# Layer 1 of a two-layer gated transformer: the last two batches as one pair instead of two single units

## The chip, the cores and the metric

The kernel runs on one core of a Trainium2 chip (trn2). The metric is the device time of one execution in microseconds (us), lower is better. The core has five instruction streams that run side by side: PE (TensorE, matrix products and transposes), DVE (VectorE), ACT (ScalarE), POOL (GpSimd) and SP (SyncE, which issues most DMAs). Each runs its own instructions strictly in the order in which they are written, and waits on semaphores that the others raise.

## The reference

Eight batches of 128 rows by 256 columns run through two layers. Cut to what matters here:

```
x = x + tanh(g_xattn[0]) * long_conv_mixer(ctx, ctx, layernorm(x))        # layer 0
x = x + tanh(g_ffn[0])   * routed_ffn(layernorm(x))                       # layer 0: router, 8 groups, silu(g) * u
x = x + tanh(g_xattn[1]) * attention(layernorm(x), ctx, mask)             # layer 1, "cross"
x = x + tanh(g_ffn[1])   * (relu(layernorm(x) @ T(w_fc))**2 @ T(w_proj))  # layer 1, "mlp"; T() = ternarized weight
```

The attention is `softmax(x ctx^T / 16 + mask) ctx`, with one head; the MLP has 640 hidden units. All is float32.

## The kernel before, in words

All of x stays on chip in the tile x_res (128 partitions = rows, then batch, then 256 columns). The work is cut into steps, such as `("down", 7)` or `("turn_1", 3)`, and every engine walks one common list of steps, `SCHEDULE`, and does its own part of each step. So the list sets the order on all engines at once. `make_schedule` builds the list: it has chains of steps (one chain per routine), each step has a number in the table `TIMES`, and the steps are sorted by it. The numbers are only sort keys, not times.

The steps that matter here:

- `warm n` lets PE do n products that nobody reads. `conv`, `fold`, `gather`, `kv` are the mixer of layer 0; `prod` is what DVE writes in a conv, `fold` is POOL's sum of it. `consts` needs the small tables (gates, the router's inverse map, mu) that SP loads.
- `chunk b c` (c = 0 to 3) are the up and gate products of the routed FFN of batch b: 12 products from line 679 and 2 from line 682. `turn_a b c` transposes the result; ACT copies it as a rounded part to a_t and DVE the remainder (`residue`, line 926). `down b` is 33 products (line 535) over the eleven tiles of a_t; the tiles 8 to 10 come from `turn_a b 3`. DVE adds the result to x_res (line 1184). Routers (`turn_top`, `flat`, `soft`, `turn_soft`) run once for each two batches, `tern_sum` belongs to the ternarized weights.
- Layer 1 runs in units, by the list `UNITS`: three pairs of batches, then batch 6 alone and batch 7 alone. A unit is a chain of 13 steps: `stat cross` (DVE statistics, POOL's rstd at line 1258), `norm cross` (DVE, xn, line 988), `turn_0` (PE transposes, ACT copies qt), `scores` (PE line 708; DVE lines 1194 and 1198; ACT exp, line 884), `turn_p` (PE, then ACT pt), `read` (PE line 720, DVE line 1209 into x_res), `stat mlp`, `norm mlp`, `turn_1` (PE, ACT rounded part and DVE remainder of x1t), `hidden` 0, 1, 2 (PE line 734; ACT relu line 904 and square line 909; DVE hsq line 1225 and the remainder hid_t line 1227), `out` (PE line 748, DVE line 1233 into x_res, then the store by SP, line 523).
- Almost each of these steps waits for the one ahead of it in its unit. `stat cross` of a unit waits for the `down` of its last batch. `hidden 0` of a unit may not stand before the `out` of the unit before it, since both use hid_t. PSUM has eight banks, given out in turn by `plan_psum`; after `down 7` five of them serve all steps.

The width of a step grows with the unit: with one batch, `hidden` has 20 products with 128 moving columns; with two it has 20 products with 256 columns:

```
                    n = P * len(UNITS[u])
                    for i, j in enumerate(range(2 * jp, min(2 * jp + 2, JT))):
                        for kt in range(2):
                            for part in range(2):
                                last = pe.matmul(psum(step)[:, i * n:(i + 1) * n],
                                                 fc_t[:, kt, j * P:(j + 1) * P], x1t[:, part, kt, 0:n],
```

Of the kernel before, what the change touches and what calls it, by code (L numbers as in the profile page):

```python
# [46 lines left out]
DONE_TILES = [range(0, 2), range(2, 5), range(5, 8), range(8, 11)]  # L47
WORDS = {"gate": 0, "up": 1}
TERNARY = ["fc", "proj"]
UNITS = [range(0, 2), range(2, 4), range(4, 6), range(6, 7), range(7, 8)]  # L50


RING_LOADS = ["gate0", "gate1", "gate2", "up0", "up1", "up2", "down0", "down1"]
# [6 lines left out]

WARMS = [13, 1, 0]
TIMES = {
    "weights": [92, 133, 137, 157, 169, 185, 211, 279, 279, 279, 281, 281, 281, 292, 296, 309, 313, 313, 327, 338,
        342, 358, 358, 358, 380, 391, 409],
    "consts": [105],
# [9 lines left out]
    "mask": [656],  # L77
    "ternary": [724, 760, 764, 807, 813, 838, 851, 863, 863, 867, 880, 921, 921, 946],
    "chunks": [547, 575, 592, 628, 656, 667, 698, 716, 736, 760, 784, 804, 836, 856, 888, 918, 924, 956, 972, 988,
        1008, 1034, 1034, 1054, 1068, 1094, 1100, 1120, 1137, 1160, 1170, 1192],  # L80
    "turns": [590, 593, 644, 660, 694, 704, 720, 740, 768, 796, 820, 844, 878, 900, 911, 927, 938, 980, 1000, 1008,
        1026, 1042, 1062, 1070, 1085, 1102, 1124, 1146, 1164, 1180, 1196, 1206],
    "downs": [689, 740, 844, 932, 1009, 1076, 1148, 1220],
# [9 lines left out]
}  # L93


def make_schedule():
# [7 lines left out]
    def router(r):  # L104
        return one_by_one((kind, "moe", r) if kind in ("stat", "norm") else (kind, r) for kind in (
            "stat", "norm", "turn_x", "logits", "top", "turn_top", "flat", "soft", "turn_soft"))

    def layer1(u):
        return one_by_one([("stat", "cross", u), ("norm", "cross", u), ("turn_0", u), ("scores", u), ("turn_p", u),
                           ("read", u), ("stat", "mlp", u), ("norm", "mlp", u), ("turn_1", u), ("hidden", u, 0),  # L110
                           ("hidden", u, 1), ("hidden", u, 2), ("out", u)])
# [24 lines left out]
    chains.update((f"router{r}", router(r)) for r in range(RUNITS))  # L136
    chains.update((f"unit{u}", layer1(u)) for u in range(len(UNITS)))
    timed = []
    for name, pieces in chains.items():
        timed += [(t, len(timed) + k, piece) for k, (t, piece) in enumerate(zip(TIMES[name], pieces, strict=True))]  # L140
        assert TIMES[name] == sorted(TIMES[name])
    start = [("warm", WARMS[0]), ("stat", "mix", 0), ("turn_ctx", 0, 0), ("turn_ctx", 0, 1), ("norm", "mix", 0),
             ("kv", 0, 0), ("warm", WARMS[1]), ("turn_q", 0, 0), ("turn_q", 0, 1), ("kv", 0, 1), ("warm", WARMS[2])]
    return start + [step for _, _, piece in sorted(timed) for step in piece]


def check_order(schedule):
# [5 lines left out]
    for b in range(B):  # L153
        for c in range(NCH):
            assert at["chunk", b, c] < at["turn_a", b, c]
        assert at["turn_a", b, NCH - 1] < at["down", b]
    for u, bs in enumerate(UNITS):
        assert at["down", bs[-1]] < at["stat", "cross", u]
# [23 lines left out]
def plan_psum():  # L182
# [19 lines left out]
    for i, step in enumerate(SCHEDULE):  # L202
        kind = step[0]
        if kind == "read":
            reads[kind] = len(UNITS[step[1]])
        if kind == "conv":
# [32 lines left out]
def batches_of(which, k):  # L239

    if which == "mix":
        return range(k * Q, (k + 1) * Q)
    return range(k * RQ, (k + 1) * RQ) if which == "moe" else UNITS[k]

# [15 lines left out]
def build(nc, x, ctx_rows, mask, g_xattn, g_ffn, kernel_rev, skip, gate_w, mask_up_w, gate_p, up_p, down_p, inv_map,  # L260
# [156 lines left out]
    def wait_drained(eng, key, reads=None):  # L417

        bank, _, before, n = USES[key]
        eng.wait_ge(drained[bank], before + (n if reads is None else reads))  # L420
# [50 lines left out]
    with block:  # L471

        @block.sync
        def _(sp):
# [39 lines left out]
            for n in range(3, len(RING_LOADS)):  # L514
# [5 lines left out]
                         w_proj.rearrange("(r p) j -> p r j", p=P)).then_inc(tern_loaded[1], 16)  # L520
            for u, bs in enumerate(UNITS):
                wait_drained(sp, ("out", u))
                sp.dma_start(out[bs.start:bs.stop].rearrange("b p l -> p b l"),
                             x_res[:, bs.start:bs.stop, :]).then_inc(stored, 16)
            sp.wait_ge(stored, 16 * len(UNITS))

# [789 lines left out]
```

## Time and profile before

| | before |
|---|---|
| median of 3 timed runs | 274.08 us (272.95 to 274.17) |
| the profiled execution, by the same clock as the runs | 271.08 us |
| its span in the trace (first to last instruction or landing) | 269.4 us |
| PE busy | 238.3 us (88%) |
| DVE busy | 184.8 us (69%) |
| ACT busy | 111.4 us (41%) |
| POOL busy | 73.4 us (27%) |
| mean TensorE clock granted, as a share of 2.4 GHz | 0.959 |

The profile is of one execution. All times inside it are counted from the start of its span. A busy share is an average over stages: what counts for a change is which engine is waited for in the stage in which it lies.

### The profile page before, as it was taken

The numbers are of one execution on the slowest core, as the hardware profiler recorded it, in microseconds if no ns is written. First come the engines' busy times: TensorE is split into PE (matmuls) and PEld (weight loads), VectorE is DVE, ScalarE is ACT, GpSimd is POOL, SyncE is SP. The second block draws the span as 40 slices with busy tenths as digits, with TensorE's granted clock in tenths as the row PEclk, the third lists the DMA queues.
The fourth block names the chain that finished last, engine by engine and source line by source line (L and its number), as shares of the span: only waits on it lengthen the run. The fifth ranks groups of instructions, "written<-read, shape, count | busy, mean of one in ns | idle before, by whom it ended". The sixth has DMA issues, their size and how long they took to land.

```text
span 269.4 us, 4600 instructions
## 1 busy us (share of the span) xinstructions
PE 238.3 (88%) x1580; PEld 225.3 (84%) x1580; DVE 184.8 (69%) x515; ACT 111.4 (41%) x229; POOL 73.4 (27%) x92
## 2 busy tenths in 40 slices
PE   7496789978789999999798799999999999996883
PEld 7495679868579998999788799999899999985873
DVE  2359999798995889686786484662764756685442
ACT  0602326840103263654444945373521771363331
POOL 1667687049586201000443110100011001102100
PEclk9889999999999999999799999999999999999566
DMA  4698527000000041000000000000000000101000
GB/s 159 190 350 191 156 58 217 1 0 1 4 0 0 2 134 63 0 1 2 0 0 2 0 0 4 1 2 0 0 24 17 2 0 4 39 0 39 4 19 19
DMA packets 14038, 11.50 MB, mean 43 GB/s; under 512 B 2912, under 2 KB 13760, under 8 KB 14016
## 3 DMA queue, kind: packets, MB, share of 16 engines
q1 hardware_dynamic: 13920, 11.16, 13.7%
q8 instruction: 13, 0.21, 0.3%
q10 hardware_dynamic: 96, 0.05, 0.1%
q14 instruction: 9, 0.07, 0.1%
HBM read 10.14 MB, written 1.07 MB: 42 GB/s over the span
## 4 chain that ended last, share of the span: by engine, by line
issue 39%; PE 30%; DVE 16%; POOL 7%; ACT 5%; DMA 1%; ACTq 0%; DVEq 0%; POOLq 0%
PE bank L679 10%; PE bank L535 6%; PE bank L542 3%; POOL kv L1280 2%; DVE prod L1007 2%; PE bank L580 2%; POOL rstd L1258 2%; DVE w_split L926 2%; PE bank L748 2%; PE bank L734 2%; ACT ctx_ext L757 2%; PE bank L582 2%; PE bank L581 2%; PE bank L682 2%; DMA x_res<-in_x 1%
## 5 line engine op out<-in xcount | busy, mean ns | idle before, releaser
L679 PE MATMUL bank<-w_split,xt 128*128 128x352 f32 x384 | 70.9, 334 | 0.0
L679 PEld LDWEIGHTS bank<-w_split,xt 128*128 128x128 f32 x384 | 62.7, 192 | 0.1
L1254 POOL TENSOR_SCALAR ve<-mv 128x2 f32<-128x2 f32 (+2 forms) x16 | 3.6, 227 | 149.2 <-DVE mv L966 149.2
L1173 DVE SCALAR_TENSOR_TENSOR act<-silu,scal,bank 128x176 f32<-128x176 f32 x64 | 22.6, 394 | 22.9 <-ACT silu L871 20.7
L535 PE MATMUL bank<-d_split,a_t 128*128 128x256 f32 x264 | 34.2, 286 | 0.0
L535 PEld LDWEIGHTS bank<-d_split,a_t 128*128 128x128 f32 x264 | 32.3, 191 | 0.5 <-DVE a_t L926 0.4
L871 ACT ACTIVATE silu<-bank 128x352 f32<-128x352 f32 x32 | 14.8, 464 | 35.2 <-PE bank L682 35.0
L1280 POOL TENSOR_TENSOR kv<-ctx_ext 128x880 f32<-128x880 f32 x16 | 27.5, 1720 | 3.0 <-ACT ctx_ext L757 2.2
L1291 POOL TENSOR_TENSOR fold<-prod 128x256 f32<-128x256 f32 x32 | 23.3, 742 | 18.3 <-DVE prod L1010 16.4
L580 PE MATMUL bank<-kv,toe 128*128 128x208 f32 x64 | 18.5, 371 | 9.5 <-DVE prod L1010 3.7
L580 PEld LDWEIGHTS bank<-kv,toe 128*128 128x128 f32 x64 | 10.6, 197 | 12.7 <-issue 9.7
L757 ACT ACTIVATE a_t<-bank 128x384 fp32r<-128x384 f32 (+1 forms) x32 | 14.7, 460 | 12.2 <-PE bank L542 11.9
L1007 DVE TENSOR_TENSOR prod<-bank,q_ext 128x320 f32<-128x320 f32 x32 | 15.5, 483 | 6.1 <-PE bank L582 4.8
L926 DVE TENSOR_TENSOR a_t<-bank,a_t 128x384 fp32r<-128x384 f32 (+1 forms) x32 | 16.6, 519 | 4.2 <-ACT a_t L757 3.9
L871 ACT ACT_TABLE_LOAD x10 | 12.8, 1283 | 12.9 <-PE bank L682 12.8
L988 DVE TENSOR_SCALAR xn<-x_res,mv,rstd 128x256 f32<-128x256 f32 x32 | 12.6, 438 | 6.5 <-POOL rstd L1258 6.5
L581 PE MATMUL bank<-kv,toe 128*128 128x208 f32 x64 | 16.8, 344 | 0.0
L582 PE MATMUL bank<-kv,toe 128*128 128x208 f32 x64 | 16.8, 344 | 0.0
L734 PE MATMUL bank<-x1t,fc_t 128*128 128x256 f32 (+1 forms) x100 | 16.3, 321 | 0.0
L682 PE MATMUL bank<-m_stack,soft_t 128*128 128x352 f32 x64 | 15.8, 328 | 0.0
L734 PEld LDWEIGHTS bank<-x1t,fc_t 128*128 128x128 f32 x100 | 15.2, 228 | 0.5 <-issue 0.3
L757 ACT ACTIVATE w_split<-bank 128x512 fp32r<-128x512 f32 (+1 forms) x12 | 6.4, 568 | 22.0 <-PE bank L542 22.0
(136 smaller groups left out, 425.8 us busy)
## 6 DMA issues: line engine op xcount, KB each, us to landing
toe<-lag_rows SPq DMA_DIRECT2D x4, 512.0 KB, 5.9
ring<-in_down_p SPq DMA_DIRECT2D x2, 704.0 KB, 4.9
x_res<-in_x SPq DMA_DIRECT2D x2, 512.0 KB, 4.4
ctx<-in_ctx_rows SPq DMA_DIRECT2D x2, 512.0 KB, 5.0
ring<-in_gate_p SPq DMA_DIRECT2D x2, 512.0 KB, 8.7
ring<-in_up_p SPq DMA_DIRECT2D x2, 512.0 KB, 4.5
out_x<-x_res SPq DMA_DIRECT2D x3, 256.0 KB, 2.2
tern_w<-in_w_fc SPq DMA_DIRECT2D x1, 640.0 KB, 4.2
```

What stands on the lines that cost most here:

```text
L535: last = pe.matmul(dst, lhs(a), rhs(b), start=start and i == 0, stop=stop and i == 2)
L580: pe.matmul(y[:, 0], toe[:, h, P:2 * P], pairs(0), start=True, stop=True)
L581: pe.matmul(y[:, 1], toe[:, h, 0:P], pairs(0), start=True, stop=False)
L582: fill(pe.matmul(y[:, 1], toe[:, h, P:2 * P], pairs(1), start=False, stop=True), step)
L679: pe.matmul(psum((name, b, c))[:, 0:CW], lhs, w_split[:, w, kt, part, cols], start=i == 0, stop=False)
L734: last = pe.matmul(psum(step)[:, i * n:(i + 1) * n], fc_t[:, kt, j * P:(j + 1) * P], x1t[:, part, kt, 0:n], start=kt + part == 0, stop=kt ...
L757: return act_e.activation(dst, src, ACT.Copy)
L871: drain(act_e.activation(silu[:, n % 2, :], psum(("gate", b, c))[:, 0:CW], ACT.Silu), ("gate", b, c))
L926: drain(dve.tensor_tensor(dst, src, hi.bitcast(F32), ALU.subtract), key)
L1173: drain(dve.scalar_tensor_tensor(out=act[:, g * NI:(g + 1) * NI], in0=silu[:, n % 2, cols], scalar=scal[:, b, g:g + 1], in1=psum(("up", b, ...
L1280: pool.tensor_tensor(kv[:, n % 2], view(ctx_ext, base, [[EXT, 4 * Q], [0, TAPS], [1, SPAN]]), view(ctx_ext, base, [[EXT, 4 * Q], [1, TAPS] ...
L1291: pool.tensor_tensor(f, p4[:, :, 0:4, :], p4[:, :, 4:8, :], ALU.add).then_inc(folded, 1)
```

## The change

`UNITS` gets four pairs. The two chains of single units become one chain of double width, and the sort keys are new, in the tail and, a little, elsewhere.

```
-UNITS = [range(0, 2), range(2, 4), range(4, 6), range(6, 7), range(7, 8)]
+UNITS = [range(0, 2), range(2, 4), range(4, 6), range(6, 8)]
...
-WARMS = [13, 1, 0]
+WARMS = [13, 0, 3]
 TIMES = {
...
-    "gather0": [84, 86, 146, 194, 223, 223, 288, 333],
+    "gather0": [64, 66, 146, 194, 223, 223, 288, 333],
...
-    "unit3": [1183, 1212, 1226, 1233, 1252, 1252, 1256, 1263, 1277, 1288, 1288, 1295, 1302],
-    "unit4": [1220, 1230, 1256, 1260, 1278, 1281, 1281, 1287, 1295, 1304, 1332, 1353, 1385],
+    "unit3": [1220, 1230, 1256, 1260, 1278, 1281, 1281, 1287, 1295, 1304, 1332, 1353, 1385],
 }
```

Apart from the tail, about a dozen pairs of neighbouring steps change places in the common list (three `turn_w` steps and one `turn_ctx` ahead of a conv or kv, `gather 0 0` ahead of the fourth conv, `turn_att 1 0` ahead of `logits 1`, `tern_sum fc` ahead of `chunk 2 1`, `stat moe 3` ahead of `chunk 2 2`, `hidden 1 2` ahead of `chunk 7 0`). The one source line that goes shifts all line numbers of the kernel after by one: line 748 of before is line 747 of after.

**The tail on PE.** From `down 7` (the 33 products with d_split and a_t) to the end, first before, where act is the routed FFN's result, xn_73 the normed rows of layer 1, s_att the attention weights, and each row has its count of products:

```order
L542 MATMUL bank<-ident,act 128x128 x3
L734 MATMUL bank<-x1t,fc_t 128x256 x4
L535 MATMUL bank<-d_split,a_t 128x256 x33
L542 MATMUL bank<-ident,xn_73 128x128 x2
L708 MATMUL bank<-ctx_ext,qt 128x128 x2
L748 MATMUL bank<-proj_t,hid_t 128x256 x20
L542 MATMUL bank<-ident,s_att 128x128
...
L734 MATMUL bank<-x1t,fc_t 128x128 x20
L542 MATMUL bank<-ident,xn_73 128x128 x2
L748 MATMUL bank<-proj_t,hid_t 128x256 x10
L734 MATMUL bank<-x1t,fc_t 128x128 x20
L748 MATMUL bank<-proj_t,hid_t 128x256 x10
```

and after:

```order
L733 MATMUL bank<-x1t,fc_t 128x256 x20
L541 MATMUL bank<-ident,act 128x128 x3
L534 MATMUL bank<-d_split,a_t 128x256 x33
L747 MATMUL bank<-proj_t,hid_t 128x256 x20
L541 MATMUL bank<-ident,xn_73 128x128 x4
L707 MATMUL bank<-ctx_ext,qt 128x128 x4
L541 MATMUL bank<-ident,s_att 128x128 x2
L719 MATMUL bank<-ctx,pt 128x256 x2
L541 MATMUL bank<-ident,xn_73 128x128 x4
L733 MATMUL bank<-x1t,fc_t 128x256 x20
L747 MATMUL bank<-proj_t,hid_t 128x256 x20
```

The two chains that were interleaved are one; the `out` of unit 2 (the first 20 products with proj_t) moved ahead of `turn_0`, and the last third of unit 2's `hidden` moved ahead of the last `turn_a`. (In the trace a product of two plain float32 operands, as in `scores`, `read` and the warm steps, counts as two records.)

**The tail on DVE, ahead of `down 7`.** This is the end of unit 2's `hidden` and the last remainder of a_t, which `down 7` needs; before:

```order
L1225 TENSOR_TENSOR hsq<-relu 128x512
L1227 TENSOR_TENSOR hid_t<-hsq,hid_t 128x2x256
L926 TENSOR_TENSOR a_t<-bank,a_t 128x3x128
L1225 TENSOR_TENSOR hsq<-relu 128x256
L1227 TENSOR_TENSOR hid_t<-hsq,hid_t 128x256
L988 TENSOR_SCALAR xn_73<-x_res,mv,rstd 128x256
L1184 SCALAR_TENSOR_TENSOR x_res<-bank,tg,x_res 128x256
```

and after:

```order
L1224 TENSOR_TENSOR hsq<-relu 128x512
L1226 TENSOR_TENSOR hid_t<-hsq,hid_t 128x2x256
L1224 TENSOR_TENSOR hsq<-relu 128x256
L1226 TENSOR_TENSOR hid_t<-hsq,hid_t 128x256
L925 TENSOR_TENSOR a_t<-bank,a_t 128x3x128
L1183 SCALAR_TENSOR_TENSOR x_res<-bank,tg,x_res 128x256
```

The remainder of a_t moved behind the last two operations of `hidden`, and the norm of the single batch 6 is gone from here.

**The middle on DVE.** This is the router of batches 4 and 5 around `tern_sum fc` (lines 1067 to 1071) and `flat 2` (from line 1135), before:

```order
L1062 TENSOR_REDUCE tern<-tern_w 128x1
L1173 SCALAR_TENSOR_TENSOR act<-silu,scal,bank 128x176 x2
L1067 TENSOR_SCALAR tern<-bank 128x1
L1070 TENSOR_SCALAR tern<-tern 128x1
L1071 TENSOR_SCALAR tern<-tern 128x1
L1135 TENSOR_REDUCE scal<-bank 128x16
```

and after:

```order
L1061 TENSOR_REDUCE tern<-tern_w 128x1
L1066 TENSOR_SCALAR tern<-bank 128x1
L1069 TENSOR_SCALAR tern<-tern 128x1
L1070 TENSOR_SCALAR tern<-tern 128x1
L1172 SCALAR_TENSOR_TENSOR act<-silu,scal,bank 128x176 x2
L1134 TENSOR_REDUCE scal<-bank 128x16
```

The three small operations moved ahead of the product of silu and up.

## Rows read from the trace of the kernel before

**Rows 1.** Timeline (start us, us): last down and unit 3's, unit 4's end.
```profile
237.10 4.12 PE L535 MATMUL bank<-d_split,a_t 128*128 128x256 f32 x33
239.09 0.55 DVE L926 TENSOR_TENSOR a_t<-bank,a_t 128x384 fp32r<-128x384 f32 x1
240.01 0.43 DVE L1227 TENSOR_TENSOR hid_t<-hsq,hid_t 128x256 fp32r<-128x256 f32 x1
241.26 0.48 DVE L1184 SCALAR_TENSOR_TENSOR x_res<-bank,tg,x_res 128x256 f32<-128x256 f32 x1 [0.50 <-PE bank L535]
242.46 2.65 PE L748 MATMUL bank<-proj_t,hid_t 128*128 128x256 f32 x20
250.42 1.22 PE L720 MATMUL bank<-ctx,pt 128*128 128x256 f32 x2 [0.59 <-ACT pt L757]
251.08 4.72 PE L734 MATMUL bank<-x1t,fc_t 128*128 128x128 f32 x20
264.17 2.50 PE L748 MATMUL bank<-proj_t,hid_t 128*128 128x256 f32 x10 [1.80 <-DVE hid_t L1227]
266.71 0.48 DVE L1233 SCALAR_TENSOR_TENSOR x_res<-bank,out_scale,x_res 128x256 f32<-128x256 f32 x1 [2.60 <-PE bank L748]
```

**Rows 2.** Half-microsecond windows of PE: length, busy (count), clock, DMA share, GB/s.
```profile
250.00:250.50 0.50, 0.08 (x1) 0.92 0.00 0
260.50:261.00 0.50, 0.50 (x6) 0.84 0.00 0
```

**Rows 3.** Timeline: steps of an earlier pair, unit 2, up to its norm.
```profile
214.72 1.08 PE L708 MATMUL bank<-ctx_ext,qt 128*128 128x128 f32 x8
216.12 0.41 DVE L1194 SCALAR_TENSOR_TENSOR s_att<-bank,neg 128x256 f32<-128x256 f32 x1
217.72 0.19 ACT L884 ACTIVATION_READ_ACCUMULATOR s_att<-s_att,nmax 128x1 f32 x1
223.01 1.03 PE L720 MATMUL bank<-ctx,pt 128*128 128x256 f32 x4
224.15 0.88 DVE L1209 SCALAR_TENSOR_TENSOR x_res<-bank,rv,x_res 128x256 f32<-128x256 f32 x2 [0.18 <-PE bank L720]
225.06 0.75 DVE L960 BATCH_NORM_STATS2 stats<-x_res 128x6 f32<-128x256 f32 x2
226.49 0.71 POOL L1258 TENSOR_TENSOR rstd<-ve,mhalf 128x2 f32<-128x2 f32 x1
227.81 0.73 DVE L988 TENSOR_SCALAR xn<-x_res,mv,rstd 128x256 f32<-128x256 f32 x2
```

**Rows 4.** Timeline: the same pair from turn_1 to the end of hidden.
```profile
231.30 0.60 PE L542 MATMUL bank<-ident,xn 128*128 128x128 f32 x4
234.31 2.15 PE L734 MATMUL bank<-x1t,fc_t 128*128 128x256 f32 x16
235.60 0.60 ACT L904 ACTIVATE relu<-bank 128x512 f32<-128x512 f32 x1 [0.46 <-PE bank L734]
236.30 0.69 DVE L1225 TENSOR_TENSOR hsq<-relu 128x512 f32<-128x512 f32 x1 [0.41 <-ACT relu L904]
```

**Rows 5.** DMA issues: tensor, queue, count, KB each, median us to landing.
```profile
out_x<-x_res SPq DMA_DIRECT2D x2, 256.0 KB, 2.2
out_x<-x_res SPq DMA_DIRECT2D x2, 128.0 KB, 1.7
```

**Rows 6.** Timeline: the router of batches 4 and 5.
```profile
125.00 0.71 DVE L1173 SCALAR_TENSOR_TENSOR act<-silu,scal,bank 128x176 f32<-128x176 f32 x2 [1.10 <-ACT silu L871]
126.17 0.29 DVE L1135 TENSOR_REDUCE scal<-bank 128x16 f32<-128x128 f32 x1
129.75 0.66 PE L542 MATMUL bank<-ident,soft_parts 128*128 128x128 f32 x4 [1.91 <-DVE soft_parts L1159]
130.50 3.48 PE L679 MATMUL bank<-w_split,xt 128*128 128x352 f32 x12
```

**Rows 7.** Timeline: the start, at the step consts.
```profile
22.58 0.20 ACT L767 ACTIVATE tg<-gates 128x4 f32<-128x4 f32 x1 [2.21 <-DMA mu<-in_mask_up_w]
```

More of the change, by code:

```diff
@@ L57 @@
              "down0": ("turn_down", 5), "down1": ("turn_down", 5)}
-WARMS = [13, 1, 0]
+WARMS = [13, 0, 3]
 TIMES = {
-    "weights": [92, 133, 137, 157, 169, 185, 211, 279, 279, 279, 281, 281, 281, 292, 296, 309, 313, 313, 327, 338,
-        342, 358, 358, 358, 380, 391, 409],
+    "weights": [92, 133, 137, 148, 160, 176, 202, 279, 279, 279, 281, 281, 281, 292, 296, 309, 313, 313, 327, 338,
+        342, 358, 366, 366, 380, 391, 409],
     "consts": [105],
[2 rows of a table removed]
[2 rows of a table added]
     "conv0": [55, 59, 62, 66, 66, 104, 122, 138, 158, 163, 184, 196, 222, 230, 258, 280],
[2 rows of a table removed]
[2 rows of a table added]
     "kv1": [338, 354, 399, 419, 460, 483, 520, 552],
     "conv1": [404, 404, 415, 447, 447, 452, 468, 484, 500, 512, 528, 542, 560, 576, 605, 608],
[2 rows of a table removed]
[2 rows of a table added]
     "mask": [656],
-    "ternary": [724, 760, 764, 807, 813, 838, 851, 863, 863, 867, 880, 921, 921, 946],
-    "chunks": [547, 575, 592, 628, 656, 667, 698, 716, 736, 760, 784, 804, 836, 856, 888, 918, 924, 956, 972, 988,
+    "ternary": [724, 756, 756, 807, 813, 838, 851, 863, 863, 867, 880, 921, 921, 942],
+    "chunks": [547, 575, 592, 628, 656, 667, 698, 711, 736, 760, 784, 804, 836, 856, 888, 918, 924, 956, 972, 988,
         1008, 1034, 1034, 1054, 1068, 1094, 1100, 1120, 1137, 1160, 1170, 1192],
-    "turns": [590, 593, 644, 660, 694, 704, 720, 740, 768, 796, 820, 844, 878, 900, 911, 927, 938, 980, 1000, 1008,
-        1026, 1042, 1062, 1070, 1085, 1102, 1124, 1146, 1164, 1180, 1196, 1206],
+    "turns": [590, 593, 644, 660, 694, 704, 720, 740, 768, 796, 820, 844, 878, 900, 911, 927, 938, 976, 1000, 1008,
+        1026, 1042, 1062, 1070, 1085, 1102, 1124, 1146, 1164, 1180, 1196, 1220],
     "downs": [689, 740, 844, 932, 1009, 1076, 1148, 1220],
     "router0": [348, 384, 420, 448, 448, 480, 480, 508, 528],
[1 row of a table removed]
[1 row of a table added]
     "router2": [676, 684, 708, 723, 734, 753, 764, 773, 784],
[1 row of a table removed]
[1 row of a table added]
     "unit0": [787, 831, 865, 872, 896, 902, 902, 964, 976, 997, 1044, 1045, 1068],
[1 row of a table removed]
[1 row of a table added]
     "unit2": [1080, 1082, 1116, 1128, 1140, 1152, 1154, 1168, 1184, 1200, 1204, 1212, 1240],
[2 rows of a table removed]
[1 row of a table added]
 }
```

16 rows, old and new, of the table TIMES are left out of this document.

## The prediction

> **What bounds the kernel now.** I read the page first. TensorE is busy 88% of the span and is granted 0.959 of its full clock of 2.4 GHz in the mean; the missing part lies mostly in the last 20 us. So there are two regimes. Up to the last `down` the kernel is a packed stream on PE. Behind it lies a tail with almost nothing to fill: two chains of dependent steps, batch 6 alone and batch 7 alone, where each step waits for another engine. I read that stretch next in the timeline and in half-microsecond windows. `down 7` starts at 237.10 and DVE takes its result at 241.26; the last `out` starts at 264.17, its addition at 266.71, and the span ends at 269.4 [rows 1]. That is 28.1 us for layer 1 of two batches, and the change is there. The clock in it: full until 250.42 (a mean of 0.92 in the window from 250.0), half (1.2 GHz) until 260.66 (0.84 in the window from 260.5) [rows 2], then full for `hidden` of batch 7, and half again for its `out`, ten products in 2.50 us [rows 1].
>
> **The tail after, step by step.** I lay the pair's chain out from rows of unit 2, which is a pair, at the full clock. An instruction that waits for another engine starts 0.05 to 0.1 us behind it, which the gaps between the rows show (the `out` of 2.65 us from 242.46, ended 245.11, was picked up at 245.15).
>
> First, `down 7` itself. In the change the last remainder of a_t stands behind the two operations of hidden on DVE. Before, it ran at 239.09, the two behind it ended at 240.44 [rows 1]. DVE has no gap there, so the remainder now ends at about 240.5. `down` needs it for its 25th product, at 237.10 + 24 x 0.125 = 240.1. It stalls some 0.45 us and ends near 241.7.
>
> Then, with the duration and the handover of each step:
> - addition to x_res, 241.80 + 0.52 = 242.32: statistics of both batches start.
> - statistics to norm: from 225.06 to the end of rstd at 227.20, plus 0.11 = 2.25 [rows 3]: 244.57. The norm of two, 0.73 [rows 3]: PE's `turn_0` at 245.35. The `out` of unit 2 (2.65 us [rows 1]) fills this wait, 241.75 to 244.4, and costs nothing. Uncovered it would cost its 2.65.
> - `turn_0`, 0.60 for four transposes [rows 4] + 0.10; ACT's copy of 512 columns 0.60 (as the relu of that width [rows 4]) + 0.05: `scores` at 246.70, 1.08 + 0.12. The mask addition starts at 247.90; from its start to the end of both exps is 217.91 - 216.12 = 1.79 [rows 3]: 249.69.
> - `turn_p` and the copy of pt, 0.93 together (two transposes, then a copy of 256 columns; half of `turn_0` and its copy, 0.68, bounds it from below, the whole, 1.35, from above): `read` at 250.62. `read` to the addition: 224.15 - 223.01 = 1.14; addition to statistics 225.06 - 224.15 = 0.91; statistics to norm 2.25; norm and handover 0.78: `turn_1` at 255.70 [rows 3].
> - `turn_1` 0.70, ACT 0.64, DVE's remainder 0.74 (0.69 as the DVE operation of that width [rows 4]): `hidden` at 257.78.
> - `hidden` to `out`: to relu 235.60 - 234.31 = 1.29, to hsq 0.70, and from the start of hsq at 236.30 to the end of hid_t at 240.44 = 4.14, less 0.47 for the a_t operation that stood between, plus 0.05 [rows 1, 4]: 5.71. `out` at 263.5.
> - `out` 2.65 + 0.04, addition of 512 columns 0.75: 266.9. Behind the last addition the span has now 269.4 - 267.19 = 2.2 us for a store of 128 KB; the store becomes 256 KB, and those took 0.5 us longer [rows 1, 5]: 2.7. End 269.6.
>
> So at the full clock the pair ends where the two singles end, at half clock for most of their tail. The clock decides. In before, PE was half idle from 245 and fell to half at 250.42. In the pair PE has from the end of `scores` at 247.8 only 0.4 us of transposes, 1 us of `read` and 0.6 of `turn_1` until 257.8, one wait of about 4 us among them (`read` to `turn_1`). I take it that the clock falls at the latest there, and price that by rows at half: `read` 1.22 for two records at 250.42, against 1.03 for four: +0.5 for two, +1.0 for four. `turn_1` +0.1. `hidden` to `out` +0.9 (eight products at 0.25 us, from 2.50 for ten, in place of 0.13). That puts `out` at 263.5 + 2.0 = 265.5. `out` at half is 20 x 0.25 = 5.0 us in place of 2.65 [rows 1]. Whether it runs at half is open: the stream of `hidden` may raise the clock, as the stream of 257.13 to 260.66 did in before. With `out` at full the span ends at 265.5 + 2.65 + 3.5 = 271.7, at half at 274.0. I take the middle, 272.8: **+3.4 us** on the tail, bounds +0.2 (all full) and +4.6.
>
> One rule speaks for the pair. A product of the single unit with 128 columns took 4.72 / 20 = 0.236 us at half clock, nearly as long as one with 256 columns (2.50 / 10 = 0.25) [rows 1]; so the pair saves 20 products x 0.236 = 4.7 us of PE time at half. By the Trainium skill, "TensorE: Matmul & The Clock Gate", section "Wait — 56ns, not 53.3ns?", products follow each other by their columns over 1.2 GHz on a cold array, which would be 107 and 213 ns and no saving at all. The row disagrees for 128 columns, and the sum goes by the row. The saving is real and is in the sum: but it pays for a start of `hidden` 7 us later than unit 3's (251.08), since nothing overlaps `down 7` any more.
>
> **The rest.** Router of batches 4 and 5: PE waits 1.91 us for soft_parts [rows 6]. DVE's chain to it starts at 126.17, 0.46 behind the end of the act product at 125.71; in the change the small operations run in the 1.10 us hole ahead of act. PE's own `tern_sum` comes 0.2 earlier and pushes the chunk by that. Net -0.2 to -0.4: I take **-0.3**. If the clock drop behind it also stayed away (12 products took 3.48 us from 130.50; at the 0.18 us of a full-clock one they are 2.2), 1.3 to 1.6 more, a rival below.
>
> Start: three warm products instead of one, later, may hold the clock through the first convs, which run at half from about 12 to 14.9. Worth up to 1.4 us there, but at 22.58 ACT was still waiting for the DMA of mu [rows 7], and DVE's `consts` needs the same landing and holds all DVE work behind it. What is won before 22.58 is lost there: 0, bounds -1.4 and +0.3 (the warm products ahead of the first conv). The other swaps of neighbours move work under a busy PE: 0, bounds -0.3 and +0.3 by the size of one a_t operation.
>
> **Sum.** 269.4 + 3.4 - 0.3 = 272.5, +3.1 on the span. The profiled execution took 271.08, 3.0 less than the median of 274.08. Part of that gap will be clock, and executions in which before's second `hidden` also runs at half (4.72 for 2.94) pay up to 1 us more in the tail (part is under the DVE chain). So the difference of the medians should be smaller: I take +2.3, **276.4 us**.
>
> **The rivals.** (1) Forecast: tail at half clock for `read` and `hidden`, `out` partly: +1.4 to +4.3. Chance 0.62. (2) The clock comes back early or falls late: tail +0.2 to +1.5; with -0.3 the time is 274 to 275.3, no change that can be told. The 256-column stream that raised the clock at 260.66 speaks for it, the long wait ahead of `turn_1` against. 0.22. (3) Faster: the wait at 127.84 in the router is what counts. If DVE's chain is ready by 127.9, the 1.91 us go, and with them the half clock from 130.95, 1.6: -3.5. It decides if the tail then costs under 2.1 us: 274.08 + 1.0 - 3.5 = 271.6. Against it: the swap moves that chain by 0.46 at most. With all other ways to be faster, 0.16. (4) That the change does little because `down 7` still sets everything is part of (2): the work behind it is a chain that nobody else covers.
>
> A measurement of this kernel can tell about 0.5% (1.4 us) from no change. Slower by over 0.5% 0.62, within 0.22, faster 0.16. The range runs from 272.8, where (2) meets (3), to 278.8, where all bounds of the tail are at their end: 274.08 + 4.6.
>
> **What the profile after would show.** `down 7` a little longer (4.5 against 4.12) with the a_t remainder near 240 in before's time; `hidden` of unit 3 starting 16 to 17 us behind the end of `down 7` as one chain with no PE work in between; products of `hidden` and perhaps `out` at 0.25 us; a wait of PE for xn of about 4 us ahead of `turn_1`; the last store with 256 KB. Wrong would be: the clock at full from `hidden` on, a shorter hop from `read` to `turn_1`, or the wait of 1.91 us at 127.84 gone.

## The result and the profile after

Before and after ran in turn on one chip, 17 times each. The median went from 272.35 us (271.16 to 274.17) to 274.95 us (274.42 to 276.81): a ratio of 1.0106, with a 95% interval of 1.0084 to 1.0128. (Here and below a ratio comes from the single runs and not from the two medians, so it can differ a little from their quotient.) The change makes the kernel 1.1% slower. The three runs of before that stood ahead of the prediction had a median of 274.08; over 17 it is 272.35.

| | before | after |
|---|---|---|
| profiled execution | 271.08 us | 274.94 us |
| its span | 269.4 us | 273.2 us |
| start of `down 7` | 237.10 | 236.19 |
| from there to the end of the span | 32.3 | 37.0 |
| PE busy | 238.3 us | 235.2 us |
| mean granted clock | 0.959 | 0.961 |

So in these two traces the body (all that is ahead of `down 7`) is 0.9 us shorter and the tail 4.7 us longer. PE is busy 3.1 us less, and it does not help.

The tail of after in the timeline (start us, us, engine, line, operation), the lines that answer to [rows 1, 3, 4]:

```profile
236.19 3.11 PE L534 MATMUL bank<-d_split,a_t 128*128 128x256 f32 x24
...
239.06 0.55 DVE L925 TENSOR_TENSOR a_t<-bank,a_t 128x384 fp32r<-128x384 f32 x1
239.66 1.34 PE L534 MATMUL bank<-d_split,a_t 128*128 128x256 f32 x9 [0.37 <-DVE a_t L925]
240.84 2.56 PE L747 MATMUL bank<-proj_t,hid_t 128*128 128x256 f32 x20
241.04 0.48 DVE L1183 SCALAR_TENSOR_TENSOR x_res<-bank,tg,x_res 128x256 f32<-128x256 f32 x1 [1.43 <-PE bank L534]
...
244.67 0.65 PE L541 MATMUL bank<-ident,xn 128*128 128x128 f32 x4 [1.27 <-DVE xn L987]
...
246.07 1.19 PE L707 MATMUL bank<-ctx_ext,qt 128*128 128x128 f32 x8 [0.75 <-ACT qt L756]
...
249.22 0.69 PE L541 MATMUL bank<-ident,s_att 128*128 128x128 f32 x2 [1.96 <-ACT s_att L883]
...
250.44 2.07 PE L719 MATMUL bank<-ctx,pt 128*128 128x256 f32 x4 [0.53 <-ACT pt L756]
...
256.57 1.11 PE L541 MATMUL bank<-ident,xn 128*128 128x128 f32 x4 [4.06 <-DVE xn L987]
...
259.16 3.92 PE L733 MATMUL bank<-x1t,fc_t 128*128 128x256 f32 x20 [1.47 <-DVE x1t L925]
...
262.03 0.69 DVE L1224 TENSOR_TENSOR hsq<-relu 128x512 f32<-128x512 f32 x1 [2.92 <-ACT relu L903]
...
265.87 3.96 PE L747 MATMUL bank<-proj_t,hid_t 128*128 128x256 f32 x20 [2.80 <-DVE hid_t L1226]
269.87 0.75 DVE L1232 SCALAR_TENSOR_TENSOR x_res<-bank,out_scale,x_res 128x512 f32<-128x512 f32 x1 [4.06 <-PE bank L747]
```

Read the brackets, which give an engine's idle time ahead of the row and what ended it: from `turn_0` at 244.67 on, every step of PE has a wait ahead of it, each for the step before it in the one chain. The longest, 4.06 us, lies between `read` and `turn_1`, as forecast.

The same stretch of after in windows (length, busy us of PE, PEld, DVE, ACT, POOL with counts, granted clock, DMA share, GB/s):

```profile
241.00:248.40 7.40, 4.24 (x33) 3.61 (x31) 3.73 (x10) 1.99 (x3) 0.94 (x2) 1.00 0.11 35
248.40:255.00 6.60, 2.76 (x6) 1.46 (x6) 2.20 (x8) 1.15 (x5) 0.26 (x2) 0.50 0.00 0
255.00:262.00 7.00, 3.95 (x17) 3.55 (x18) 1.43 (x3) 1.20 (x2) 0.68 (x1) 0.50 0.01 2
262.00:265.40 3.40, 1.08 (x9) 0.87 (x8) 3.20 (x6) 2.55 (x5) 0.00 (x0) 0.99 0.01 2
265.40:268.80 3.40, 2.93 (x13) 2.93 (x14) 0.42 (x1) 0.00 (x0) 0.00 (x0) 0.51 0.00 0
268.80:273.20 4.40, 1.04 (x8) 0.83 (x7) 0.75 (x1) 0.00 (x0) 0.00 (x0) 0.89 0.18 60
```

The clock is at 1.2 GHz from 248.4 to 262.0, so for `turn_p`, `read`, `turn_1` and most of `hidden`; it is at 2.4 GHz while DVE finishes hidden and PE waits; and at 1.2 again for the first three quarters of `out`.

The start and the router, which answer to [rows 6, 7], timeline of after:

```profile
22.63 0.21 ACT L766 ACTIVATE tg<-gates 128x4 f32<-128x4 f32 x1 [3.01 <-DMA mu<-in_mask_up_w]
22.63 0.15 DVE L933 TENSOR_SCALAR pidx<-pidx 128x1 int32<-128x1 int32 x1 [0.88 <-DMA mu<-in_mask_up_w]
...
125.58 0.71 DVE L1172 SCALAR_TENSOR_TENSOR act<-silu,scal,bank 128x176 f32<-128x176 f32 x2 [1.01 <-ACT silu L870]
...
126.21 0.28 DVE L1134 TENSOR_REDUCE scal<-bank 128x16 f32<-128x128 f32 x1
...
129.93 0.66 PE L541 MATMUL bank<-ident,soft_parts 128*128 128x128 f32 x4 [1.62 <-DVE soft_parts L1158]
...
130.67 2.23 PE L678 MATMUL bank<-w_split,xt 128*128 128x352 f32 x12
```

DVE reaches `consts` 0.88 us ahead of the DMA now and waits for it there. PE's wait for soft_parts is 1.62 us, not 1.91, and the 12 products behind it take 2.23 us, not 3.48: here the clock stayed up.

### The profile page after: what moved, and what is told of

It is laid out like the page before. It is cut to its first block, busy times and chain, and to the rows that moved or that the text cites. A ratio compares the mean times of both kernels' runs of the same rounds, so it can differ in the third digit from the quotient of the medians.

```text
span 273.2 us, 4515 instructions
## 1 busy us (share of the span) xinstructions
PE 235.2 (86%) x1564; PEld 221.3 (81%) x1564; DVE 182.4 (67%) x503; ACT 110.3 (40%) x220; POOL 72.2 (26%) x88
## 4 chain that ended last, share of the span: by engine, by line
issue 40%; PE 33%; DVE 13%; DMA 4%; SPq 3%; POOL 3%; ACT 3%; POOLq 0%; DVEq 0%; ACTq 0%
PE bank L678 9%; PE bank L534 7%; PE bank L541 4%; PE bank L579 3%; PE bank L580 2%; PE bank L581 2%; DMA mu<-in_mask_up_w 2%; POOL rstd L1257 2%; PE bank L681 1%; DMA x_res<-in_x 1%; PE bank L747 1%; SPq L492 1%; DVE stats L959 1%; DVE m_stack L1054 1%; DVE prod L1006 1%
## 5 line engine op out<-in xcount | busy, mean ns | idle before, releaser
L678 PE MATMUL bank<-w_split,xt 128*128 128x352 f32 x384 | 69.5, 330 | 0.0
L678 PEld LDWEIGHTS bank<-w_split,xt 128*128 128x128 f32 x384 | 61.5, 188 | 0.1
L1253 POOL TENSOR_SCALAR ve<-mv 128x2 f32<-128x2 f32 (+1 forms) x14 | 3.3, 233 | 152.9 <-DVE mv L965 152.9
L534 PEld LDWEIGHTS bank<-d_split,a_t 128*128 128x128 f32 x264 | 32.3, 191 | 1.0 <-DVE a_t L925 1.0
L1006 DVE TENSOR_TENSOR prod<-bank,q_ext 128x320 f32<-128x320 f32 x32 | 15.5, 483 | 5.0 <-PE bank L581 4.1
L541 PE MATMUL bank<-ident,xn 128*128 128x128 f32 x64 | 10.2, 286 | 7.6 <-DVE xn L987 7.6
L681 PE MATMUL bank<-m_stack,soft_t 128*128 128x352 f32 x64 | 15.5, 323 | 0.0
L541 PE MATMUL bank<-ident,act 128*128 128x128 f32 x88 | 15.1, 276 | 0.4 <-DVE act L1172 0.3
L959 DVE BATCH_NORM_STATS2 stats<-x_res 128x6 f32<-128x256 f32 x32 | 11.8, 416 | 5.2 <-DMA x_res<-in_x 4.9
```

The lines of the kernel that those rows point to most:

```text
L534: last = pe.matmul(dst, lhs(a), rhs(b), start=start and i == 0, stop=stop and i == 2)
L541: last = pe.transpose(psum(key)[0:cols, k * rows:(k + 1) * rows], piece, ident[0:rows, 0:rows])
L678: pe.matmul(psum((name, b, c))[:, 0:CW], lhs, w_split[:, w, kt, part, cols], start=i == 0, stop=False)
L681: fill(pe.matmul(psum((name, b, c))[:, 0:CW], soft_t[half][:, c // 2, rows], m_stack[:, w, cols], start=False, stop=True), (name, b, c))
L1006: drain(dve.tensor_tensor(o[:, :, 0:TAPS, :], view(y, 0, [[YW, 2 * Q], [SPAN, TAPS], [1, HD]]), view(q_ext, qb + 3, [[EXT, 2 * Q], [1, TAP ...
```

## The experiments

My theory was: the loss is the tail alone, in two parts, a longer chain and the half clock, with the clock deciding how much. The rivals: the clock hardly matters and the chain is all; or the order ahead of the tail has a share. Three more questions: what in the chain is longer, what the stall in `down 7` costs, and whether the start is worth 0. Ratios are to the kernel before on the same chip, with 95% intervals; the last three runs (`single_late2`, `pair_warm_at`, `best_plain`) were on another chip than the rest. Lengths of the tail in the traces run from the start of `down 7`, which takes the body out.

**The tail alone.** Units and tail of after, everything ahead as before.

```
-UNITS = [range(0, 2), range(2, 4), range(4, 6), range(6, 7), range(7, 8)]
+UNITS = [range(0, 2), range(2, 4), range(4, 6), range(6, 8)]
-    "unit3": ..., "unit4": ...
+    "unit3": as after; the last number of "turns" 1220
```

> The kernel before with the pair and its tail alone; all steps ahead of the tail, and the warm products at the start, stay as before. My theory: the whole loss lies in the tail, and the other swaps gave about 0.9 us back, so this is the slowest version, 3 to 4.5 us over the kernel before. Rival (the swaps elsewhere are worth nothing, or cost): then it stands where the full change stands, 2.6 us over before, or under it.

276.29 us, ratio 1.0164 (1.0124 to 1.0204): 4.4 us slower by the ratio, the slowest of all, as expected. In its trace the tail is 37.1 us (236.62 to 273.7), as in after.

**The body alone.** The kernel after with the five units and the tail of before.

```
-UNITS = [range(0, 2), range(2, 4), range(4, 6), range(6, 8)]
+UNITS = [range(0, 2), range(2, 4), range(4, 6), range(6, 7), range(7, 8)]
-    "unit3": as after
+    "unit3": ..., "unit4": as before; the last number of "turns" 1206
```

> The kernel after with five units and the old tail; the order ahead of the tail and the warm products are those of after. My theory: 0.3 to 1.5 us faster than before, from the router's wait near 128 us and from a clock drop there that comes less often. Rival (the swaps only fitted the pair's tail): same as before within 0.3 us.

270.51 us, ratio 0.9960 (0.9941 to 0.9978): 1.1 us faster. The two parts add up within their intervals: +4.4 - 1.1 = +3.3, against +2.9 by the ratio of the full change. The rival that the swaps fit only the pair's tail falls. Not all of the 1.1 us is the order, though; more on that below.

**The pair with the clock held.** The kernel after, with products whose result nobody reads in PE's waits of the tail.

```
+TAIL_WARMS = {("scores", 3): 5, ("read", 3): 10, ("turn_1", 3): 3, ("hidden", 3, 2): 7}
...
+    return [s for step in steps for s in ([step, ("warm", TAIL_WARMS[step])] if step in TAIL_WARMS else [step])]
```

> The kernel after with products that nobody reads in PE's four waits of the tail (5 behind scores, 10 behind read, 3 behind turn_1, 7 behind hidden), so that the clock has no reason to fall; the chain itself is as it was. My theory (chain plus half clock): read, turn_1, hidden and out run at full, 1.0 + 0.4 + 0.9 + 1.4 = 3 to 3.7 us less than after. Rival (the tail is long only because its steps stand in a row, and the clock hardly matters): less than 1 us. A third outcome, slower than after, would say that the unread products stand in the chain's way.

270.93 us, ratio 0.9988 (0.9963 to 1.0012), so about 3.2 us under after by the two ratios. The clock was at full until the last `out` was done. Its tail in the timeline:

```profile
234.44 3.11 PE L536 MATMUL bank<-d_split,a_t 128*128 128x256 f32 x24
...
248.45 1.13 PE L721 MATMUL bank<-ctx,pt 128*128 128x256 f32 x4 [0.53 <-ACT pt L758]
249.42 2.39 PE L552 MATMUL bank<-ident,ones 128*128 128x128 f32 x20
...
253.64 0.66 PE L543 MATMUL bank<-ident,xn 128*128 128x128 f32 x4 [1.83 <-DVE xn L989]
...
255.77 2.65 PE L735 MATMUL bank<-x1t,fc_t 128*128 128x256 f32 x20 [0.80 <-DVE x1t L927]
...
261.62 2.66 PE L749 MATMUL bank<-proj_t,hid_t 128*128 128x256 f32 x20 [1.64 <-DVE hid_t L1228]
264.32 0.75 DVE L1234 SCALAR_TENSOR_TENSOR x_res<-bank,out_scale,x_res 128x512 f32<-128x512 f32 x1 [2.75 <-PE bank L749]
```

Behind the unread products PE still waits for the chain's next step each time (1.83 us ahead of `turn_1`, 0.80 ahead of `hidden`, 1.64 ahead of `out`), so they are not in the chain's way; `read` is 1.13 for 2.07, `hidden` 2.65 for 3.92, `out` 2.66 for 3.96. From the start of `down 7` to the end of the span at 267.6 it is 33.2 us, where it was 37.0.

**The single units with the clock held.** The kernel before, with the same kind of products.

```
+TAIL_WARMS = {("scores", 4): 4, ("turn_p", 4): 1, ("turn_1", 4): 2, ("hidden", 4, 2): 4}
```

> The kernel before with such products in its waits (4 behind the last scores, 1 behind the last turn_p, 2 behind the last turn_1, 4 behind the last hidden). My theory: with the clock held, the single units win more than the pair, since they have twice the products: hidden of batch 6 2.9 for 4.7 us, both outs 1.2 less each, read and transposes 0.6: 4 to 5 us less than before, so the single units stay ahead of the pair. Rival (the single units only suffer from narrow products, which the clock does not change): 1 to 2 us less, and the pair with its clock held draws level.

266.60 us, ratio 0.9834 (0.9792 to 0.9877): 4.5 us faster than before, as expected (4 to 5). With the clock held on both sides the single units are 1.5% under the pair (0.9834 against 0.9988), and they have the slower body. The timeline:

```profile
236.07 4.12 PE L537 MATMUL bank<-d_split,a_t 128*128 128x256 f32 x33
...
240.03 0.38 PE L544 MATMUL bank<-ident,xn 128*128 128x128 f32 x2
...
249.75 2.53 PE L736 MATMUL bank<-x1t,fc_t 128*128 128x128 f32 x20
...
260.73 1.45 PE L750 MATMUL bank<-proj_t,hid_t 128*128 128x256 f32 x10 [0.86 <-DVE hid_t L1229]
262.22 0.48 DVE L1235 SCALAR_TENSOR_TENSOR x_res<-bank,out_scale,x_res 128x256 f32<-128x256 f32 x1 [1.54 <-PE bank L750]
```

From `down 7` to the end of the span at 264.9 it is 28.8 us, 4.4 less than the pair at the same clock. `turn_0` of batch 6 follows `down 7` at once: that is the head start of batch 6, whose statistics and norm were done while `down 7` still ran.

**Without the head start.** The single units with held clock again, but batch 6's statistics and norm wait for `down 7`, and the `out` of unit 2 stands ahead of `turn_0`, as in the pair.

```
-    "unit3": [1183, 1212, ...
+    "unit3": [1220, 1221, ...
     "unit2": last number 1240 -> 1222
```

> The version with single units and held clock, but the statistics and the norm of batch 6 wait for the last down, and the out of unit 2 stands ahead of turn_0, as in the pair. It takes from the single units only their head start over the last down. Theory 1 (the head start is what the pair lost, some 3 us): 2.5 to 3.5 us over the version with held clock, so near the pair with held clock, 1.3% over it. Theory 2 (the narrow steps are what counts: each step of a chain of one batch is shorter, and two chains fill each other's waits): under 1.5 us over it.

271.11 us, ratio 0.9976 (0.9940 to 1.0013): over the version with head start by 3.9 us by the ratios and 4.5 by the medians, more than the 2.5 to 3.5 expected. Its clock fell twice in the tail (at 248 and 258), so this is not the head start alone. It leaves the size open, and was repeated with more unread products:

```
-TAIL_WARMS = {("scores", 4): 4, ("turn_p", 4): 1, ("turn_1", 4): 2, ("hidden", 4, 2): 4}
+TAIL_WARMS = {("turn_0", 3): 1, ("scores", 3): 4, ("turn_p", 3): 1, ("turn_0", 4): 1, ("scores", 4): 4,
+              ("turn_p", 4): 1, ("turn_1", 4): 4, ("hidden", 4, 2): 4}
```

> The version without the head start once more, with unread products also in the waits of batch 6's chain, since the clock had fallen twice in its tail. With the clock held: batch 6's hidden starts 2.9 us later than with the head start (seen in the trace of the version before), and the end follows: 2.5 to 3.2 us over the version with single units and held clock. If it is over by 4 us or more with the clock at full, something else is in it; under 1.5 us, the head start is not what the pair lost.

268.67 us, ratio 0.9908 (0.9872 to 0.9945): 2.0 us over the version with head start by the ratios, under the 2.5 to 3.2 expected; the two intervals just overlap. Its profiled execution had a clock of 1.0:

```profile
235.00 4.12 PE L537 MATMUL bank<-d_split,a_t 128*128 128x256 f32 x33
...
241.74 0.44 PE L544 MATMUL bank<-ident,xn 128*128 128x128 f32 x2 [0.23 <-DVE xn L990]
...
250.53 2.53 PE L736 MATMUL bank<-x1t,fc_t 128*128 128x128 f32 x20
...
261.50 1.45 PE L750 MATMUL bank<-proj_t,hid_t 128*128 128x256 f32 x10 [0.86 <-DVE hid_t L1229]
```

`hidden` of batch 6 starts 15.5 us behind the start of `down 7`, against 13.7 with head start: 1.8 us, and the last `out` is 1.8 later too (26.5 against 24.7). In the first try `hidden` of batch 6 starts 16.4 us behind the start of `down 7` (236.04 to 252.42), 2.7 us over the version with head start; the expectation above says 2.9. That first figure had half clock in it, which is why the forecast from it was too high. So the head start is worth 1.8 us in the trace and about 2 in the runs.

**The stall in `down 7`.** The last `turn_a` again ahead of the last third of unit 2's hidden, first in the kernel after, then in the pair with held clock.

```
-    "turns": [..., 1196, 1220],
+    "turns": [..., 1196, 1206],
```

> The kernel after with the last turn_a again ahead of the last third of unit 2's hidden. It takes away the stall in the last down that the prediction put at 0.45 us. If the stall is on the path, 0.2 to 0.5 us less than after; if out of unit 2 and the statistics hide it, nothing.

274.80 us, ratio 1.0110 (1.0064 to 1.0157) against after's 1.0106: no difference that can be told. The clock of the single executions lay between 0.950 and 0.968 and spread them over 2.8 us.

> The pair with held clock, and the last turn_a ahead of the last third of hidden. With the clock out of play the stall of 0.36 us in the last down should show: 0.2 to 0.5 us less than the pair with held clock. Nothing, if the statistics behind it absorb it.

269.92 us, ratio 0.9937 (0.9904 to 0.9970) against 0.9988 (0.9963 to 1.0012). The intervals overlap at their ends. The trace shows it:

```profile
235.60 4.12 PE L536 MATMUL bank<-d_split,a_t 128*128 128x256 f32 x33
239.56 2.56 PE L749 MATMUL bank<-proj_t,hid_t 128*128 128x256 f32 x20
243.39 0.66 PE L543 MATMUL bank<-ident,xn 128*128 128x128 f32 x4 [1.27 <-DVE xn L989]
...
262.10 2.66 PE L749 MATMUL bank<-proj_t,hid_t 128*128 128x256 f32 x20 [1.64 <-DVE hid_t L1228]
```

The last `out` starts 26.5 us behind the start of `down 7`, not 27.2 (234.44 to 261.62). With the clock at full in both tails the stall costs 0.7 us, more than the 0.2 to 0.5 expected.

**The start.** The kernel after with the warm products of before.

```
-WARMS = [13, 0, 3]
+WARMS = [13, 1, 0]
```

> The kernel after with the warm products of before (one ahead of turn_q, none behind). The prediction put the new ones at 0 us, because DVE waits for the DMA of mu at 22.6 anyway: the same as after within 0.3 us, though the clock falls during the first convs. Rival: 0.5 to 1.4 us slower than after, if the convs' time gets through.

274.75 us, ratio 1.0136 (1.0088 to 1.0184) against 1.0106 (1.0084 to 1.0128). The runs can't tell them apart to better than 0.4%. The trace can: its clock fell at 12.1 to half, its first `prod` came 0.8 us later than in after (14.46, 13.64), and DVE began `consts` at 22.69 against 22.63. (Further on that trace is ahead of after, 235.37 against 236.19 at `down 7`, with a fall of after's clock near 71 us in between that this one does not have; so only the stretch up to `consts` can be compared.)

**The best version.** Single units, the body of after, the unread products, and batch 6's first `hidden` ahead of batch 7's norm; and the same without that swap.

```
-    "unit3": [..., 1288, 1288, 1295, 1302],   "unit4": [..., 1281, 1287, 1295, ...
+    "unit3": [..., 1288, 1289, 1295, 1302],   "unit4": [..., 1281, 1288, 1295, ...
```

> The good parts together: single units with the old tail, the order of after ahead of it, products that nobody reads in the waits of the tail, and the first third of batch 6's hidden ahead of batch 7's norm on DVE, which waits 0.9 us for rstd there while the relu is ready. Order ahead of the tail 0.8, clock 4.5 (both measured), swap 0.3 to 0.8: 5.5 to 6 us under before, 1.6 to 2.2%. If the swap only delays batch 7, it stands at 5 us or above.

265.56 us, ratio 0.9781 (0.9743 to 0.9820): 2.2% faster than before, the fastest of all, and 5.9 us where 5.5 to 6 were expected.

> The best version without the swap of batch 6's hidden and batch 7's norm. Tells what the swap gave: the hidden chain's hsq started 0.8 us earlier with it and the last out 0.45 us, so 0.3 to 0.6 us over the best. It has the same order ahead of the tail as the pair with held clock, and is the fair comparison for it: 3.6 us under it if the chain is what costs.

268.89 us, ratio 0.9893 (0.9856 to 0.9930). That is 3 us over the version with the swap and 1.6 over the single units with the body of before, where I had forecast 0.3 to 0.6 over the best. Against the pair with held clock, which has the same order ahead of the tail, it is 2.6 us faster by the ratios, where 3.6 were expected. The end of batch 6 in the trace, first with the swap:

```profile
254.84 1.45 PE L750 MATMUL bank<-proj_t,hid_t 128*128 128x256 f32 x10 [0.56 <-DVE hid_t L1229]
256.13 2.35 PE L736 MATMUL bank<-x1t,fc_t 128*128 128x128 f32 x20
```

and without it:

```profile
255.90 1.84 PE L750 MATMUL bank<-proj_t,hid_t 128*128 128x256 f32 x10 [1.48 <-DVE hid_t L1229]
257.54 4.36 PE L736 MATMUL bank<-x1t,fc_t 128*128 128x128 f32 x20
```

Without the swap the clock fell at 256.8, inside batch 6's `out` and 0.9 us behind PE's wait of 1.48 us, and the second `hidden` took 4.36 us, not 2.35. The granted clock of its executions was 0.965 to 0.986, that of the version with the swap 0.984 to 1.0. The swap cuts the wait to 0.56 us.

What the swap is worth without the clock can be read from the record. At full clock the last `out` starts 24.7 us behind the start of `down 7` without the swap (`single_warm`) and 23.8 with it (236.52 to 260.28). And at a granted clock of 0.984 executions took 267.02 and 267.12 us without it and 266.15 with it (on two chips). So about 0.9 of the 3 us is the swap itself, more than the 0.3 to 0.6 forecast, and the rest is clock. That the shorter wait is what kept the clock is not shown: `single_warm` has the same wait of 1.48 us and kept its clock in its trace, `single_late` has it and lost it.

## Why the prediction was right, and where not

Forecast: slower, 276.4 us; measured 274.95. The direction and the mechanism held: one dependent chain with nothing beside it, at half clock for most of it. Its sizes did not all hold, and the sentence that weighed the two causes did not either.

**The chain.** Most handovers came as priced: statistics to norm 2.25 and 2.25, mask to the end of the exps 1.79 and 1.79, `read` at half 2.14 and 2.18, `hidden` to relu 2.2 and 2.17, store 2.7 and 2.6. Two terms were too small: the stall of `down 7`, 0.45 against 0.7, and the transposes at half clock (`turn_p` to `read` 0.93 against 1.22, `turn_1` to ACT 0.8 against 1.21). `out` was put in the middle between full and half, 3.8; it took 3.96. So `hidden` started 18.2 us behind the end of `down 7`, not 16 to 17, and 9.0 us later than unit 3's when both are counted from `down 7`, not 7.

**The size of the tail.** +3.4 us were forecast; it is +4.7 in the two traces, 0.1 beyond the bound of 4.6 that I gave, and +4.4 in the runs of the tail alone. The 1.3 us that are missing against the traces lie half in the chain and half in the clock. At full clock I had the span end 32.5 us behind the start of `down 7` (237.10 to 269.6); the pair with held clock took 33.2. And I put 3.2 us for the half clock, where 3.8 were measured (37.0 - 33.2).

**The size of the body.** It was taken at -0.3 us; it gave -0.9 in the traces and -1.1 in the runs. Part of that is clock. With no fall of the clock ahead of the tail, `down 7` started at 235.00 with the order of before (`single_late2`) and at 234.44 with that of after (`pair_warm`): 0.6 us. The runs agree: at a granted clock of 0.952 to 0.955 the kernel before took 271.35 us in the mean (15 runs), the body alone 270.77 (6 runs). So the order is worth about 0.6 us, and what is above that is clock.

The two errors have opposite signs and partly cancel in the sum (+3.1 forecast on the span, +3.8 measured); that is luck. On the medians +2.3 was forecast, +2.6 measured. That the medians differ by less than the two traces was foreseen, with the reason that the second `hidden` of the kernel before can run at half clock in other executions and cost up to 1 us. The trace of the body alone shows such an execution: its second `hidden` took 4.36 us for 2.94, and its tail 33.2 us for 32.3. The absolute time was 1.5 us off because it stood on a median of before, from three runs, that was 1.7 us too high.

**The step that was wrong** is the sentence "The clock decides": I compared the pair at full clock (269.6) with single units at half clock and found them equal. At the same clock they are not. The full clock takes 3.8 us from the pair's tail (37.0 to 33.2) and 3.5 from the singles' (32.3 to 28.8), and the distance is 4.7 without and 4.4 with it. The half clock is a cost of both; the choice of units is a matter of the chain. Its 4.4 us, all at full clock, by differences of single traces:

| | us |
|---|---|
| stall in `down 7` (27.2 - 26.5) | 0.7 |
| head start of batch 6 over `down 7` (26.5 - 24.7) | 1.8 |
| last `out`, addition and store of two batches, from the start of `out`: 261.62 to 267.6 = 6.0, against 261.50 to 265.6 = 4.1 | 1.9 |

What is left is equal: from the start of `down 7` to the last `out`, the pair without the stall and the single units without the head start both take 26.5 us. One chain of wide steps is as long here as two chains of narrow ones that fill each other's waits. PE time, on which pairing saves, is not what this stretch waits for. (It saved less than the prediction's 4.7 us, too: the 20 products that stay are the wider ones, 0.25 us for 0.236, and the second `hidden` of before took 2.94 us, most of it at full clock. PE was busy 3.1 us less.)

**The rest.** The start was worth 0 in the trace for the reason given: DVE waits 0.88 us at `consts` for the DMA. In the router the wait shrank by 0.29 us, as forecast. Behind it the profiled execution of after kept its clock and that of before did not; the trace of the tail alone, which has the old order there, kept it too (12 products in 2.15 us from 131.00), so the new order is not shown to be the cause. The rival that was to make the kernel faster, the whole wait gone, did not occur.

## What to carry to other kernels

What this case shows: at the end of a kernel, count the chain and not the engine time: what starts ahead of the last long producer, and how much is left behind the last wait (the last product, addition and store), matter more than wide instructions. Split the last work so that its last piece is small. Before you blame the clock for a difference, hold it on both sides: products that nobody reads, put into waits that are longer than they are, gave 1.2% to the pair here and 1.7% to the single units.

## What had not been expected

Single executions of one kernel differ by their granted clock, and the time follows it: of the pair with its clock held, those at a clock of 0.998 and above took 269.4 to 270.3 us, those at 0.980 to 0.986 271.9 to 272.5. The places of such falls ahead of the tail moved: among the eight traces with the order of after there, one has none, and the others fell near 10, 12, 22, 28 or 71 us, two of them twice; with the order of before it was near 12, 24, 71 or 131, or nowhere. Each lasted about 4 us, and one such fall put the start of `down 7` back by 0.9 to 1.8 us against the trace without one. So one profile does not say which waits of the body cost clock, and two profiles that differ by a microsecond at `down 7` do not say which order is better.

In `consts` one small DVE operation is long in the traces of before, after and the start experiment, and not always the same one: in after a CAST of 128x3 took 1.63 us from 22.88, while POOL's kv ran from 22.76 for 1.73; in the start experiment a TENSOR_SCALAR of 64x64 took 1.60 us from 23.99. In both the operation ends within 0.1 us of the end of the kv that POOL runs beside it (24.51 and 24.49, 25.59 and 25.54). That DVE waits for POOL there was not tested.
